# Output projection and routing's row scaling merged into one phase pipelined by tile, with the first expert weights loaded during attention

## The chip, the cores and the metric

One Trainium2 chip, one of its cores. The metric is device time in microseconds of one execution of the whole program; times shown as a median are over several runs on the chip.

## What is computed

The reference takes x of 4 batches x 1024 rows x 256 features (4096 rows in all, float32) through four layers, each added to its own input: a causal attention with 16 heads of 16 features, a mixture of experts (8 experts, 2 per row, hidden size 512), a second attention with one head of 256 features, and the same mixture of experts again:

```python
x = x + attn_a(layernorm(x))      # 16 heads of 16, causal, over 1024 rows of a batch
x = x + ffn(layernorm(x))         # rms norm, top 2 of 8 experts, swiglu 256 -> 512 -> 256
x = x + attn_b(layernorm(x))      # one head of 256, not causal, output layernorm
x = x + ffn(layernorm(x))
```

The part that the change touches lies between the first attention and the first experts: the heads' rows are divided by their softmax sums, multiplied by `Wo` and added to x; then x is normalised (n), x becomes x + n (the outer and the inner residual of the layer), and t = n x (rms scale) x `norm_scale` is what the experts and the router read; the router's logits are t times an 8-column matrix.

## The kernel before

The rows are held as 32 tiles of 128 rows in `g["X"]`, [128, 32, 256], in on-chip memory from start to end. The program is a row of phases (`phase` in `program`, from L1908); each is a block in which every engine has its own instruction list, and the next begins when all engines have ended the last. In time order: `project_qkv`, `attend_a`, `project_out`, `scale_rows`, `rank`, `experts`, then `layer_b`, `rank`, `experts` for the other two layers.

`attend_a` (L361) goes through U = 16 units of four heads and one batch, with a loop (`rotating`, L69). SyncE (SP) issues, in step u: the six head loads of unit u+2 (`load_heads`, L106), then the copy of that unit's V from `g["V"]` into one of three buffers `Vst` (`load_v`, L408), then, once VectorE has the row maxima of unit u+1, three small DMAs that put them into `Qst` (`max_rows`, L414). Each head load is split in three parts of n = 3, 2, 1 (`Q_RUNS`): K and Q are stored as bfloat16 parts, and a Q part is repeated n times by a broadcast on the DRAM side:

```python
q_part = qk_dram[0, bass.ds(u, 1), r * DK:(r + 1) * DK, :, :].rearrange("u d h t -> u d (h t)")   # L109
sp.dma_start(g["Qst"][c * DK:(c + n) * DK, s, :, :].rearrange("p h t -> p (h t)"),                # L112
             q_part.broadcast_to([n, DK, HG * S])).then_inc(g["kq_in"], 16)
```

ScalarE stores each unit's result to `o_dram`, [16 units, 128, 1024]: four heads of 32 rows each, of which 17 hold something, the 16 features and the softmax sum.

`project_out` (L628) takes one tile a step. SP loads the tile's [128, 4, 128] block of `o_dram` into one of two buffers `Ot` (L654), waiting for the transposes two tiles back; in every second step it also issues one piece of each expert matrix, 512 KB of the first (`w1`, L658) and 256 KB of the second (`w2`, L661). TensorE makes four 128 x 128 transposes (L688), VectorE takes the inverse of the sums (L717) and multiplies (L719), TensorE transposes again (L673), ScalarE copies (L704), TensorE multiplies by `Wo` (L679), VectorE adds into X (L712) and takes the statistics (L724); their aggregates for all 32 tiles come at the end (L736).

`scale_rows` (L739) starts with two roots on ScalarE (L777) for all tiles at once, and then per tile: n on VectorE (L806), t on VectorE (L814), x + n on POOL (L852), two transposes of t (L840), a copy on ScalarE (L781), and the logits on TensorE (L830). SP stores t and x in groups of four tiles (L763, L766) and one more tile (L768).

`rank` (L855) starts by loading the gate's bias (L900) and computes on VectorE which row goes to which expert. `experts` (L1058) waits for all expert weights before its first product.

## Time and profile before

| what | us |
|---|---|
| median of 3 runs | 1978.02 |
| lowest and highest of them | 1974.34, 1983.2 |
| the profiled execution's own time | 1974.66 |
| span of its trace | 1972.9 |

The profile is of one execution of its own. Its rows are read as follows: an engine's busy time is the time in which it had an instruction under way; the clock (PEclk) is the clock granted to TensorE as a share of 2.4 GHz; the DMA share is the mean busy share of the core's 16 DMA engines. Rows by line give the count, the busy time, the mean of one, and behind the second bar the idle time just ahead of them on their engine with what ended it.

### The profile page before, as it was taken

To read this page: it belongs to the slowest core of one execution; us is meant where nothing else is said; L and a number is where in the kernel's file an instruction comes from. 1 tells how busy PE (TensorE), PEld (TensorE's weight loads), DVE (VectorE), ACT (ScalarE), POOL (GpSimd) and SP (SyncE) were. 2 spreads that over 40 slices of the span, in tenths; PEclk is the share of its full clock that TensorE was granted. 3 is DMA by queue.
4 is the path that set the end of the run, shared out by engine and by line. 5 is a ranking of instruction groups with operands and counts; after the bars stand their busy time and mean duration, and the time that the engine had idled before them with its cause. 6 is when DMAs were issued, how large, how long until landed. Compare 5 with 4: busy or idle time off the path is not lost. (4 is left out here: it accounts for less than half of the span.)

```text
span 1972.9 us, 32641 instructions
## 1 busy us (share of the span) xinstructions
PE 1750.6 (89%) x8298; PEld 974.6 (49%) x8299; DVE 1341.7 (68%) x2703; ACT 809.7 (41%) x1644; POOL 792.7 (40%) x773
## 2 busy tenths in 40 slices
PE   6979999999998567599999999599975799999997
PEld 3533443444342457266666666344543466666664
DVE  4648888888783357677777777348887567676774
ACT  2424666666666113033333333346761233333332
POOL 4331111111111005156666666134540466666663
PEclk9988999999999895599999999799985899999998
DMA  4662332433320675322222222400113222222222
GB/s 127 161 140 74 94 99 71 100 84 80 98 69 17 209 233 187 123 46 43 47 44 46 43 48 43 109 1 7 58 65 131 56 43 48 43 45 45 47 43 29
DMA packets 116268, 152.83 MB, mean 77 GB/s; under 512 B 17696, under 2 KB 98336, under 8 KB 113120
## 3 DMA queue, kind: packets, MB, share of 16 engines
q1 hardware_dynamic: 79776, 106.28, 19.3%
q0 software_dynamic: 31808, 37.32, 11.8%
q10 hardware_dynamic: 4608, 8.39, 1.2%
q8 instruction: 26, 0.43, 0.1%
q14 instruction: 50, 0.41, 0.1%
HBM read 86.47 MB, written 56.69 MB: 73 GB/s over the span
## 5 line engine op out<-in xcount | busy, mean ns | idle before, releaser
L501 DVE TENSOR_REDUCE a_mx<-a_p_sn 128x1 f32<-128x512 f32 (+3 forms) x640 | 371.2, 632 | 88.6 <-PE a_p_sn L540 61.4
L474 ACT ACTIVATE a_Pt<-a_p_st 128x512 f32<-128x512 f32 (+2 forms) x624 | 306.3, 576 | 191.2 <-PE a_p_st L554 177.1
L1202 ACT ACTIVATE e_y<-e_yb,e_wt 128x256 f32<-128x256 f32 x142 | 72.2, 508 | 505.7 <-DVE e_yb L1229 503.0
L1162 PE MATMUL e_p_y<-w,e_hT 128*128 x1136 | 270.4, 381 | 2.0 <-ACT e_hT L1196 2.0
L1141 PE MATMUL e_p_g<-w,e_tT 128*128 x568 | 270.7, 599 | 0.0
L1141 PE MATMUL e_p_l<-w,e_tT 128*128 x568 | 267.9, 594 | 0.0
L1162 PEld LDWEIGHTS e_p_y<-w,e_hT 128*128 128x128 f32 x1136 | 216.2, 191 | 92.4 <-issue 66.7
L537 PE MATMUL a_p_sn<-Kst,Qst 96*128 96x512 bf16 (+3 forms) x768 | 248.0, 343 | 7.2 <-DMA Qst<-qk_parts 5.7
L450 POOL TENSOR_SCALAR_AFFINE_SELECT a_Pt<-a_Pt 128x512 f32<-128x512 f32 x128 | 81.6, 637 | 418.7 <-ACT a_Pt L474 418.7
L554 PE MATMUL a_p_st<-Qst,Kst 99*128 99x512 bf16 (+3 forms) x768 | 214.4, 332 | 15.2 <-ACT a_Pt L474 12.5
L1053 POOL DMA_INDIRECT xs<-t_rows,token x142 | 143.5, 1011 | 134.5 <-DVE r_used L1006 83.7
L1246 DVE TENSOR_TENSOR e_lin<-e_p_l,R 128x512 f32<-128x512 f32 x142 | 98.2, 692 | 111.6 <-PE e_p_l L1141 111.6
L1242 DVE TENSOR_TENSOR e_glu<-e_p_g,R 128x512 f32<-128x512 f32 x142 | 98.2, 692 | 110.5 <-PE e_p_g L1141 89.0
L1105 POOL DMA_INDIRECT e_wt<-pick_weights,pick x142 | 153.3, 1080 | 48.3 <-issue 42.7
L1113 POOL DMA_INDIRECT x_rows<-e_y,result x71 | 115.0, 1620 | 121.7 <-ACT e_y L1202 118.6
L1113 POOL DMA_INDIRECT out<-e_y,result x71 | 115.0, 1620 | 120.1 <-ACT e_y L1202 120.1
L569 PE MATMUL a_p_o<-a_Pt,a_Vst 128*32 128x512 f32 (+3 forms) x1536 | 160.8, 500 | 0.9 <-POOL a_Pt L450 0.9
L537 PEld LDWEIGHTS a_p_sn<-Kst,Qst 96*128 96x128 bf16 x768 | 75.8, 99 | 147.3 <-DVE a_mx L501 118.3
L1141 PEld LDWEIGHTS e_p_g<-w,e_tT 128*128 128x128 f32 x568 | 98.0, 192 | 69.3 <-issue 69.0
L1141 PEld LDWEIGHTS e_p_l<-w,e_tT 128*128 128x128 f32 x568 | 97.4, 191 | 70.0 <-issue 70.0
L554 PEld LDWEIGHTS a_p_st<-Qst,Kst 99*128 99x128 bf16 x768 | 68.9, 98 | 111.7 <-ACT a_Pt L474 77.5
L1785 PE MATMUL b_p_s<-b_nT,b_gT 128*128 128x512 f32 x256 | 117.9, 607 | 2.8 <-ACT b_p_s L1457 2.8
(211 smaller groups left out, 2534.8 us busy)
## 6 DMA issues: line engine op xcount, KB each, us to landing
qk_parts<-a_part SPq DMA_DIRECT2D x64, 192.0 KB, 2.7
a_Vst<-V SPq DMA_DIRECT2D x16, 512.0 KB, 16.5
o_rows<-a_OT ACTq DMA_DIRECT2D x32, 256.0 KB, 2.1
a_Ot<-o_rows SPq DMA_DIRECT2D x32, 256.0 KB, 3.4
w<-in_mlp SPq DMA_DIRECT2D x16, 512.0 KB, 4.2
R<-in_mlp_b SPq DMA_DIRECT2D x16, 512.0 KB, 8.2
Kst<-qk_parts SPq DMA_DIRECT2D x16, 384.0 KB
Qst<-qk_parts SPq DMA_DIRECT2D x16, 384.0 KB
```

The lines of the kernel that those rows point to most:

```text
L474: act.activation(weights(kb, slice(h, h + n), a, b), p_st[:, i % RING, 0:n * (b - a)].rearrange("p (n w) -> p n w", n=n), ACT.Exp, scale=D ...
L501: dve.tensor_reduce(mx[:, hs[0]:hs[-1] + 1, place], p_sn[:, (s + k) % RING, 0:w * len(hs)].rearrange("p (h w) -> p h w", w=w), AX.X, ALU.m ...
L537: mm = pe.matmul(out, Qst[0:ROWS, s, h, qb * P:(qb + 1) * P], Kst[0:ROWS, s, h, k0:k0 + kw], start=True, stop=True, skip_group_check=True)
L554: mm = pe.matmul(p_st[:, i % RING, j * (b - a):(j + 1) * (b - a)], Kst[0:ROWS + MROWS, s, h0 + j, kb * P:(kb + 1) * P], Qst[0:ROWS + MROWS ...
L569: mm = pe.matmul(p_o[PAD * h:PAD * (h + 1), c, a:512], Vst[:, s, kb, PAD * h:PAD * (h + 1)], weights(kb, h, 512 * c + a, 512 * (c + 1)), s ...
L1053: pool.indirect_dma_start(out=g["xs"][:, j % 2, :], out_offset=None, in_=t_dram, in_offset=bass.IndirectOffsetOnAxis(ap=g["token"][:, j:j ...
L1105: pool.indirect_dma_start(out=wt[:, j:j + 1], out_offset=None, in_=w_dram, in_offset=bass.IndirectOffsetOnAxis(ap=g["pick"][:, j:j + 1], a ...
L1113: pool.indirect_dma_start(out=acc, out_offset=bass.IndirectOffsetOnAxis(ap=g["result"][:, j:j + 1], axis=0), in_=y[:, j % 2, :], in_offset ...
L1141: mm = pe.matmul(bank[:, s, :], tT[:, s, k * P:(k + 1) * P], g["w1"][:, bass.ds(e, 1), k, cols].rearrange("p a n -> p (a n)"), start=(k == ...
L1162: mm = pe.matmul(p_y[:, s, 0:D], hT[:, s, k * P:(k + 1) * P], g["w2"][:, bass.ds(e, 1), k, :].rearrange("p a n -> p (a n)"), start=(k == 0 ...
L1242: dve.tensor_tensor(glu[:, s, :], p_g[:, s, :], bias(0), ALU.add).then_inc(g_read, 1)
L1785: mm = pe.matmul(p_s[:, j % 2, half, :], gT[:, k, q * P:(q + 1) * P], nT[:, b % 2, k, half * 512:(half + 1) * 512], start=(k == 0), stop=( ...
```

## The change

It does four things. The first expert matrix is loaded during attention, one piece of 512 KB a step, into the memory of the V of a unit whose copy has been made: V and `w1` share `g["VW"]`. `project_out` and `scale_rows` become one phase, `out_rows`, in which each engine goes through 41 steps and works on several tiles at different stages in each. The moments, roots and coefficients are taken for groups of four tiles. And n is made by ScalarE from a shift and a factor, not by VectorE. The load of `Ot` now takes two tiles at a time, into one of three buffers, with four DMAs of 17 rows each in place of one of 128.

```diff
@@ -414,6 +414,15 @@
                     sp.dma_start(Qst[ROWS + r:ROWS + r + 1, s, :, :].rearrange("p h (q t) -> p (h q) t", t=P),
                                  mT[r * HG * QB:(r + 1) * HG * QB, :]).then_inc(m_in, 16)
+            def load_w1(u):
+
+                if isinstance(u, int) and u >= U - 2:
+                    sp.wait_ge(v_in, 16 * U)
+                sp.nop(nofuse=True)
+                halves = g["mlp1"].rearrange("e (k p) n -> (e k) p n", p=P)
+                sp.dma_start(g["VW"][:, bass.ds(u, 1), :].rearrange("p u n -> p (u n)"),
+                             halves[bass.ds(u, 1)].rearrange("u p n -> p (u n)")).then_inc(g["w_in"], 16)
+
             load_v(0, 0)
             max_rows(0, 0)
             sp.wait_ge(v_in, 16)
@@ -435,6 +444,7 @@
                     load_v(u + 2, (s + 2) % 3)
                 if not (isinstance(u, int) and u == U - 1):
                     max_rows(u + 1, (s + 1) % 3)
+                load_w1(u)
             rotating(sp, step)
         @block.gpsimd
@@ -625,231 +635,255 @@
-def project_out(nc, mem, g, o_dram):
...
-def scale_rows(nc, mem, g, t_dram, acc):
...
+def out_rows(nc, mem, g, o_dram, t_dram, acc):
...
@@ -1123,7 +1157,7 @@
         @block.tensor
         def _(pe):
-            pe.wait_ge(g["w_in"], 2 * 16 * NT // 2)
+            pe.wait_ge(g["w_in"], 16 * (U + NT // 2))
             def rows(j, s, first):
                 pe.wait_ge(xs_in[s], 16 * (j - s) + 32)
@@ -1918,6 +1952,9 @@
         g["st6"] = keep.sb("st6", [P, NT, 6])
         g["mv"] = keep.sb("mv_all", [P, NT, 2])
         g["mv2"] = keep.sb("mv2_all", [P, NT, 2])
+        g["VW"] = keep.sb("values_then_w1", [P, U, QB * HG * PAD])
+        g["V"] = g["VW"][:, :, :].rearrange("p u (k h c) -> p u k h c", h=HG, c=PAD)
+        g["w1"] = g["VW"][:, :, :].rearrange("p (e k) n -> p e k n", k=KD)
         g["token"] = keep.sb("token", [P, MT], I32)
         g["result"] = keep.sb("result", [P, MT], I32)
         g["pick"] = keep.sb("pick", [P, MT], I32)
@@ -1935,20 +1972,17 @@
         with ExitStack() as heads:
             early = Mem(nc, heads)
-            g["V"] = early.sb("V", [P, U, QB, HG, PAD])
             g["Kst"] = early.sb("Kst", [P, 3, HG, S], BF16)
             g["Qst"] = early.sb("Qst", [P, 3, HG, S], BF16)
             phase(project_qkv, "a1_", a["x"], qk_dram)
             phase(attend_a, "a2_", qk_dram, o_dram)
         g["R"] = keep.sb("R", [P, NT, D])
         g["xs"] = keep.sb("xs", [P, 2, D])
-        g["w1"] = keep.sb("w1", [P, E, KD, 2 * I])
         g["w2"] = keep.sb("w2", [P, E, KI, D])
-        phase(project_out, "a3_", o_dram)
         g["xs_in"] = [keep.sem(f"xs_in1_{s}") for s in range(2)]
         with ExitStack() as span:
             g["p_l"] = Mem(nc, span).ps("p_logits1", [P, 512])
-            phase(scale_rows, "s1_", t_dram, x_dram)
+            phase(out_rows, "a3_", o_dram, t_dram, x_dram)
             phase(rank, "r1_", t_dram, w_dram)
         phase(experts, "e1_", t_dram, w_dram, x_dram, spent, True)
         g["xs_in"] = [keep.sem(f"xs_in2_{s}") for s in range(2)]
```

The new function, with the declarations cut:

```python
def out_rows(nc, mem, g, o_dram, t_dram, acc):
    C = DK + 1
    DEEP, GROUP = 3, 4
    Ot = mem.sb("Ot", [HG * C, DEEP, HG, 2 * P])
    ...
    p_l = g["p_l"]
    STEPS = NT + 9
    def n_of(j):
        return g["R"][:, j % 8, :]
    def t_of(j):
        return g["R"][:, 8 + j % 8, :]
    def x_of(j):
        return g["X"][:, j, :]
    with nc.Block() as block:
        @block.sync
        def _(sp):
            def load(q):
                if q >= DEEP:
                    sp.wait_ge(rows_done, 2 * (q - DEEP) + 2)
                b, at = 2 * q // QB, 2 * q % QB * P
                for h in range(HG):
                    src = o_dram[b * HG:(b + 1) * HG, PAD * h:PAD * h + C, at:at + 2 * P]
                    sp.dma_start(Ot[C * h:C * (h + 1), q % DEEP], src.rearrange("u p t -> p u t")).then_inc(o_in[q % DEEP], 16)
            def load_w2(i):
                e, k = i // 2, i % 2
                sp.dma_start(g["w2"][:, e, 2 * k:2 * k + 2, :], g["mlp2"][e, 2 * k * P:2 * (k + 1) * P, :]
                             .rearrange("(k p) n -> p k n", p=P)).then_inc(g["w_in"], 16)
            def store(c):
                rows = slice(GROUP * c * P, GROUP * (c + 1) * P)
                sp.wait_ge(t_done, GROUP * (c + 1))
                sp.dma_start(t_dram[rows, :].rearrange("(t p) d -> p t d", p=P),
                             g["R"][:, 8 + GROUP * (c % 2):8 + GROUP * (c % 2 + 1), :]).then_inc(t_out[c % 2], 16)
                sp.wait_ge(added, GROUP * (c + 1))
                sp.dma_start(acc[rows, :].rearrange("(t p) d -> p t d", p=P),
                             g["X"][:, GROUP * c:GROUP * (c + 1), :]).then_inc(x_out, 16)
            load(0)
            sp.dma_start(wo[:, :, :], g["WoT"].rearrange("(k p) n -> p k n", p=P)).then_inc(w_in, 16)
            load(1)
            sp.dma_start(srep[:, :], g["scale"].partition_broadcast(P)).then_inc(c_in, 16)
            sp.dma_start(gw[:, :, :], g["gate_w"].rearrange("(k p) e -> p k e", p=P)).then_inc(c_in, 16)
            for j in range(0, STEPS + 4, 2):
                if j // 2 + 2 < NT // 2:
                    load(j // 2 + 2)
                if j // 2 < NT // 2:
                    load_w2(j // 2)
                if j >= 12 and j % 4 == 0 and (j - 12) // 4 < NT // GROUP:
                    store((j - 12) // 4)
            sp.dma_start(acc[T:T + P, :], g["X"][:, 0, :]).then_inc(x_out, 16)
            for s in range(2):
                sp.wait_ge(t_out[s], 16 * (NT // 8))
            sp.wait_ge(x_out, 16 * (NT // GROUP + 1))
        @block.tensor
        def _(pe):
            def rows(j):
                pe.wait_ge(o_in[j // 2 % DEEP], 16 * HG * (j // 2 // DEEP + 1))
                if j >= 2:
                    pe.wait_ge(on_done, j - 1)
                for u in range(HG):
                    mm = pe.transpose(p_r[:, j % 2, u * HG * C:(u + 1) * HG * C],
                                      Ot[:, j // 2 % DEEP, u, j % 2 * P:(j % 2 + 1) * P], g["ident"][0:HG * C, 0:HG * C])
                mm.then_inc(rows_done, 1)
            def turn_out(j):
                pe.wait_ge(on_done, j + 1)
                if j >= 1:
                    pe.wait_ge(onT_done, j)
                for k in range(KD):
                    mm = pe.transpose(p_o[:, k * P:(k + 1) * P], On[:, j % 2, k * P:(k + 1) * P], g["ident"][:, :])
                mm.then_inc(to_done, 1)
            def multiply(j):
                pe.wait_ge(onT_done, j + 1)
                if j >= 2:
                    pe.wait_ge(x_done, j - 1)
                for k in range(KD):
                    mm = pe.matmul(p_x[:, j % 2, 0:D], OnT[:, j % 2, k * P:(k + 1) * P], wo[:, k, :],
                                   start=(k == 0), stop=(k == KD - 1))
                mm.then_inc(px_done, 1)
            def turn(j):
                pe.wait_ge(t_done, j + 1)
                if j >= 2:
                    pe.wait_ge(tT_done, j - 1)
                for k in range(KD):
                    mm = pe.transpose(p_t[:, j % 2, k * P:(k + 1) * P], t_of(j)[:, k * P:(k + 1) * P], g["ident"][:, :])
                mm.then_inc(tp_done, 1)
            def logits(j):
                pe.wait_ge(tT_done, j + 1)
                for k in range(KD):
                    mm = pe.matmul(p_l[:, E * j:E * (j + 1)], tT[:, j % 2, k * P:(k + 1) * P], gw[:, k, :],
                                   start=(k == 0), stop=(k == KD - 1), skip_group_check=True)
                mm.then_inc(l_done, 1)
            pe.wait_ge(w_in, 16)
            pe.wait_ge(c_in, 32)
            for j in range(STEPS):
                if j < NT:
                    rows(j)
                if 0 <= j - 1 < NT:
                    turn_out(j - 1)
                if 0 <= j - 2 < NT:
                    multiply(j - 2)
                if 0 <= j - 7 < NT:
                    turn(j - 7)
                if 0 <= j - 8 < NT:
                    logits(j - 8)
        @block.scalar
        def _(act):
            def out_turned(j):
                act.wait_ge(to_done, j + 1)
                if j >= 2:
                    act.wait_ge(px_done, j - 1)
                act.copy(OnT[:, j % 2, :], p_o[:, 0:D]).then_inc(onT_done, 1)
            def deviations(c):
                at = slice(GROUP * c, GROUP * (c + 1))
                act.wait_ge(mv_done, c + 1)
                act.activation(root[:, 0, at], g["mv"][:, at, 1], ACT.Sqrt, bias=g["eps"][:, :]).then_inc(root_done, 1)
                act.activation(root[:, 1, at], g["mv"][:, at, 1], ACT.Sqrt, bias=g["eps2"][:, :], scale=1.0 + EPS
                               ).then_inc(root_done, 1)
            def normal(j):
                act.wait_ge(coef_done, 2 * (j // GROUP + 1))
                if j >= 8:
                    act.wait_ge(added, j - 7)
                    act.wait_ge(t_done, j - 7)
                act.activation(n_of(j), x_of(j), ACT.Identity, scale=inv[:, 0, j:j + 1], bias=shift[:, j:j + 1]
                               ).then_inc(n_done, 1)
            def turned(j):
                act.wait_ge(tp_done, j + 1)
                if j >= 2:
                    act.wait_ge(l_done, j - 1)
                act.copy(tT[:, j % 2, :], p_t[:, j % 2, 0:D]).then_inc(tT_done, 1)
            for j in range(STEPS):
                if 0 <= j - 1 < NT:
                    out_turned(j - 1)
                if 0 <= j - 6 < NT:
                    normal(j - 6)
                if 0 <= j - 8 < NT:
                    turned(j - 8)
                if j % GROUP == 1 and 0 <= (j - 5) // GROUP < NT // GROUP:
                    deviations((j - 5) // GROUP)
        @block.vector
        def _(dve):
            def inverse_sums(j):
                dve.wait_ge(rows_done, j + 1)
                rows = p_r[:, j % 2, 0:H * C].rearrange("p (h c) -> p h c", c=C)
                dve.reciprocal(rec[:, j % 2, :], rows[:, :, DK]).then_inc(rec_done, 1)
            def attended(j):
                dve.wait_ge(rec_done, j + 1)
                if j >= 2:
                    dve.wait_ge(to_done, j - 1)
                rows = p_r[:, j % 2, 0:H * C].rearrange("p (h c) -> p h c", c=C)
                dve.tensor_tensor(On[:, j % 2, :].rearrange("p (h d) -> p h d", d=DK), rows[:, :, 0:DK],
                                  rec[:, j % 2, :].unsqueeze(2).to_broadcast([P, H, DK]), ALU.mult).then_inc(on_done, 1)
            def add(j):
                dve.wait_ge(px_done, j + 1)
                dve.tensor_tensor(x_of(j), p_x[:, j % 2, 0:D], x_of(j), ALU.add).then_inc(x_done, 1)
            def statistics(j):
                dve.wait_ge(x_done, j + 1)
                ins = dve.bn_stats(g["st6"][:, j, :], x_of(j))
                if j % GROUP == GROUP - 1:
                    ins.then_inc(st_done, 1)
            def moments(c):
                dve.wait_ge(st_done, c + 1)
                for j in range(GROUP * c, GROUP * (c + 1)):
                    ins = dve.bn_aggr(g["mv"][:, j, :], g["st6"][:, j, :])
                ins.then_inc(mv_done, 1)
            def coefficients(c):
                at = slice(GROUP * c, GROUP * (c + 1))
                dve.wait_ge(root_done, 2 * c + 2)
                dve.reciprocal(inv[:, :, at], root[:, :, at]).then_inc(inv_done, 1)
                dve.wait_ge(inv_done, c + 1)
                dve.scalar_tensor_tensor(out=shift[:, at], in0=g["mv"][:, at, 0], scalar=-1.0, in1=inv[:, 0, at],
                                         op0=ALU.mult, op1=ALU.mult).then_inc(coef_done, 1)
                dve.tensor_tensor(inv[:, 1, at], inv[:, 1, at], root[:, 0, at], ALU.mult).then_inc(coef_done, 1)
            def scaled(j):
                dve.wait_ge(n_done, j + 1)
                if j >= 8:
                    dve.wait_ge(tp_done, j - 7)
                    dve.wait_ge(t_out[j // GROUP % 2], 16 * (j // 8))
                dve.scalar_tensor_tensor(out=t_of(j), in0=n_of(j), scalar=inv[:, 1, j:j + 1],
                                         in1=srep[:, :], op0=ALU.mult, op1=ALU.mult).then_inc(t_done, 1)
            dve.wait_ge(c_in, 32)
            for j in range(STEPS):
                if j < NT:
                    inverse_sums(j)
                if 0 <= j - 7 < NT:
                    scaled(j - 7)
                if j < NT:
                    attended(j)
                if j % GROUP == 2 and 0 <= (j - 6) // GROUP < NT // GROUP:
                    coefficients((j - 6) // GROUP)
                if 0 <= j - 2 < NT:
                    add(j - 2)
                    statistics(j - 2)
                if j % GROUP == 1 and 0 <= (j - 5) // GROUP < NT // GROUP:
                    moments((j - 5) // GROUP)
        @block.gpsimd
        def _(pool):
            for j in range(NT):
                pool.wait_ge(n_done, j + 1)
                pool.tensor_tensor(x_of(j), x_of(j), n_of(j), ALU.add).then_inc(added, 1)
```

## Rows read from the trace of the kernel before

**Rows 1.** The profile page: span and busy time of each engine.
```profile
span 1972.9 us, 32641 instructions
...
PE 1750.6 (89%) x8298; PEld 974.6 (49%) x8299; DVE 1341.7 (68%) x2703; ACT 809.7 (41%) x1644; POOL 792.7 (40%) x773
```

**Rows 2.** Windows: attention, output projection, row scaling, ranking; columns in the first line.
```profile
core 0: us, PE busy (x) PEld busy (x) DVE busy (x) ACT busy (x) POOL busy (x), PEclk, DMA share, GB/s
150.00:650.00 500.00, 474.44 (x3544) 191.76 (x3543) 377.28 (x712) 317.88 (x656) 81.58 (x128) 0.98 0.31 78
650.00:740.30 90.30, 57.22 (x320) 46.52 (x320) 47.93 (x160) 11.93 (x33) 0.00 (x0) 0.90 0.77 236
740.30:784.40 44.10, 38.33 (x192) 37.73 (x192) 36.68 (x69) 13.83 (x35) 26.10 (x32) 0.50 0.58 197
784.40:821.40 37.00, 17.65 (x67) 8.96 (x67) 29.62 (x77) 1.77 (x3) 0.00 (x0) 0.50 0.34 115
```

**Rows 3.** Groups by line, 650 to 785 us: busy us, mean ns, idle before.
```profile
L852 POOL TENSOR_TENSOR X<-X,s_n 128x256 f32<-128x256 f32 x32 | 26.1, 835 | 107.9 <-DVE s_t L814 107.9
...
L688 PE MATMUL a_p_r<-ident,a_Ot 128*128 128x128 f32 x128 | 22.6, 304 | 32.2 <-DMA a_Ot<-o_rows 32.2
...
L814 DVE SCALAR_TENSOR_TENSOR s_t<-s_n,s_inv,s_srep 128x256 f32<-128x256 f32 x32 | 13.9, 473 | 0.0
L712 DVE TENSOR_TENSOR X<-a_p_x,X 128x256 f32 (+1 forms) x32 | 13.6, 425 | 6.9 <-PE a_p_x L679 3.9
L719 DVE TENSOR_TENSOR a_On<-a_p_r,a_rec 128x256 f32<-128x256 f32 x32 | 13.6, 425 | 1.1
...
L724 DVE BATCH_NORM_STATS2 st<-X (+1 forms) x29 | 12.2, 422 | 0.0
...
L717 DVE RECIPROCAL a_rec<-a_p_r 128x16 f32<-128x16 f32 x32 | 8.1, 254 | 70.8 <-PE a_p_r L688 70.7
```

**Rows 4.** Timeline where attention ends: start us, duration us, engine, line, operation.
```profile
650.04 0.43 SPq L648 DMA_DIRECT2D a_wo<-in_WoT  x1
650.52 1.38 SPq L654 DMA_DIRECT2D a_Ot<-o_rows  x2
...
654.04 1.09 PE L688 MATMUL a_p_r<-ident,a_Ot 128*128 128x128 f32 x4 [7.24 <-DMA a_Ot<-o_rows]
```

**Rows 5.** Timeline where the row scaling ends and the ranking starts.
```profile
778.76 1.58 POOL L852 TENSOR_TENSOR X<-X,s_n 128x256 f32<-128x256 f32 x2 [0.62 <-DVE s_t L814]
...
784.45 0.34 SPq L900 DMA_DIRECT2D r_gb<-in_gate_b  x1
```

**Rows 6.** Timeline of SyncE's queue for one attention step.
```profile
559.90 0.83 SPq L112 DMA_DIRECT2D Qst<-qk_parts  x1
...
561.39 0.73 SPq L112 DMA_DIRECT2D Qst<-qk_parts  x1
...
564.34 0.58 SPq L408 DMA_DIRECT2D a_Vst<-V  x1
```

**Rows 7.** Windows behind that step's issues; DMA share is of 16 engines.
```profile
565.00:570.00 5.00, 4.62 (x37) 1.76 (x34) 3.65 (x7) 3.50 (x8) 0.78 (x2) 1.00 0.76 177
570.00:575.00 5.00, 5.00 (x37) 1.77 (x33) 4.30 (x7) 3.04 (x6) 0.63 (x1) 1.00 0.19 69
575.00:580.00 5.00, 5.00 (x44) 2.13 (x41) 3.53 (x7) 2.56 (x5) 0.64 (x1) 1.00 0.12 50
```

**Rows 8.** DMA issues, whole execution: count, KB each, median us to landing.
```profile
a_Vst<-V SPq DMA_DIRECT2D x16, 512.0 KB, 16.5
...
w<-in_mlp SPq DMA_DIRECT2D x16, 512.0 KB, 4.2
```

**Rows 9.** DMA queues, 745 to 780 us: packets, MB, share of 16 engines.
```profile
q1 hardware_dynamic: 7392, 7.34, 60.9%
```

**Rows 10.** The same from 660 to 736 us.
```profile
q1 hardware_dynamic: 21005, 19.06, 80.9%
```

**Rows 11.** Waits from 150 to 648 us: total us, times, longest.
```profile
PE a_p_st L554 <- DMA Qst<-a_mT: 0.7, 1, 0.7
```

More of the change, by code:

```diff
@@ L664, in _ @@
-            paired(sp, NT, step)
-        @block.tensor
-        def _(pe):
-            pe.wait_ge(w_in, 16)
-            def turn(j, s):
-                pe.wait_ge(on_done, j + 1)
-                for k in range(KD):
-                    mm = pe.transpose(p_t[:, s, k * P:(k + 1) * P], On[:, s, k * P:(k + 1) * P], g["ident"][:, :])
-                mm.then_inc(t_done, 1)
-            def multiply(j, s):
-                pe.wait_ge(onT_done, j + 1)
-                for k in range(KD):
-                    mm = pe.matmul(p_x[:, s, 0:D], OnT[:, s, k * P:(k + 1) * P], wo[:, k, :],
-                                   start=(k == 0), stop=(k == KD - 1))
-                mm.then_inc(px_done, 1)
-            def step(j, s, first, last):
-                pe.wait_ge(o_in[s], 8 * (j - s) + 16)
-                if not first:
-                    pe.wait_ge(on_done, j - 1)
-                for u in range(HG):
-                    mm = pe.transpose(p_r[:, s, u * P:(u + 1) * P], Ot[:, s, u, :], g["ident"][:, :])
-                mm.then_inc(rows_done, 1)
-                if not (first and s == 0):
-                    turn(j - 1, 1 - s)
-                if not first:
-                    multiply(j - 2, s)
-            paired(pe, NT, step)
-            turn(NT - 1, 1)
-            for t in range(NT - 2, NT):
-                pe.wait_ge(x_done, t - 1)
-                multiply(t, t % 2)
@@ L770, in _ @@
                 sp.wait_ge(t_out[s], 16 * (NT // 8))
-            sp.wait_ge(x_out, 16 * (NT // 4 + 1))
-        @block.scalar
-        def _(act):
-            for r in range(2):
-                act.wait_ge(chain, 1 if r == 0 else 4)
-                act.activation(root[:, r, :], var1[:, :], ACT.Sqrt, bias=g["eps"][:, :]).then_inc(roots, 1)
-            for j in range(NT):
-                act.wait_ge(tp_done, j + 1)
-                act.copy(tT[:, j % 2, :], p_t[:, j % 2, 0:D]).then_inc(tT_done, 1)
```

198 lines of the change are left out of this document (71 added, 127 removed).

## The prediction, written before the changed kernel ran

> **What bounds the kernel now.** I read the page for the span [rows 1], then windows cut where the phases meet [rows 2]. Four stretches matter: the first attention, 650.04 to 740.3 us (output projection), to 784.4 (row scaling), and the ranking, which nothing in the diff touches. The change works on the two in the middle. From the projection's first issued instruction at 650.04 [rows 4] to the ranking's first at 784.45 [rows 5] they take 134.4 us.
>
> The groups by line [rows 3] say what each waits for. In the projection TensorE idled 32.2 us before the transposes of L688, released by the DMA into `Ot`, while the DMA engines were 77% busy at 236 GB/s [rows 2]: it is bound by transfers. In the scaling the DMA share is 58%, and TensorE is busy 38.33 of 44.10 us at a granted clock of 0.50, the lower of its two levels (1.2 of 2.4 GHz); it had been at 0.90 before. So an ordinary reading is: take the expert weights out of the transfer-bound phase, lay the two phases over each other, and win some tens of microseconds.
>
> The next view changes that. In every middle step of attention SyncE issues six head loads and one copy of V. Two of the six are `Qst` loads by L112 whose DRAM side is `broadcast_to([n, DK, HG*S])` with n = 3 and n = 2 [rows 6]. After all are issued the DMA share is 0.76, then 0.19, then 0.12 [rows 7]. Sixteen times 0.19 is 3.0 engines, sixteen times 0.12 is 1.9. So long after the others have finished, three engines and then two still work: just as many as n, the size of the outermost dimension on the DRAM side. And the V copy, 512 KB over 128 partitions, issued last, lands after 16.5 us, where an equal weight load lands after 4.2 [rows 8]: its share on the slow engines stands behind their backlog. If the two loads had gone to different engines, five would have been busy together. They use the same ones. The number is what one gets from the largest count up to 16 that divides the outermost dimension of both sides (48 and 3 give 3, 32 and 2 give 2, 128 and 128 give 16).
>
> The Trainium skill says this outright ("DMA: Bandwidth & Descriptors", section "Why a DMA increments its semaphore by 16 and not by 1"): the issuing side takes the largest k up to 16 that divides both slowest dimensions, on the lowest-numbered engines, and 127 partitions get one. By that, the trace agrees; by it the two phases take the 250 us worked out below, and without it the 106 of the first rival.
>
> **The change part by part.** The new `Ot` load reads only 17 of each head's 32 rows: four DMAs for two tiles, each [17, 4, 256 floats] on both sides. 17 is prime and shares no divisor with 16. So each of the four runs on one engine, and all four on the same one. That is the term that decides.
>
> *Load on that engine.* A load moves 4 x 17 x 4 = 272 pieces of 1 KB. There are 16 loads: 4352 pieces. Ahead of the last one the same engine also has its sixteenth of what is spread over all: `wo` 16, `srep` 8, thirteen of the sixteen `w2` loads 13 x 16 = 208, four pairs of stores 4 x 64 = 256. Sum 4840 pieces; `gw`'s 16 pieces of 32 bytes I leave at nothing.
>
> *Price of a piece.* From 745 to 780 us only 1 KB pieces moved: 7.34 MB in 60.9% of 16 x 35 us = 341 us of engine time, 47.6 ns per 1024 bytes [rows 9]. From 660 to 736, with half-size pieces in the mix, 19.06 MB took 80.9% of 16 x 76 = 984 us, or 52.9 ns [rows 10]: the upper bound. The two engines alone from 575 to 580 moved 50 GB/s, 26 GB/s each, with much larger pieces: 39.4 ns [rows 7], the lower bound. I take 47.6, the row with pieces of this size. 4840 x 47.6 = 230.4 us; the bounds are 190.7 and 255.8.
>
> *Is the engine ever idle?* Three buffers are in turn. `load(q)` waits for the transposes of pair q-3, which come within a few us of that pair's landing; two loads, some 26 us of work, are then still queued. So it is always fed. It even delays the start: TensorE first waits for `srep` and `gw`, which stand behind two loads on that engine, (544 + 24) x 47.6 ns = 27 us. That lies beside the 230.4 and costs nothing more.
>
> *The ends.* First issue to first piece about 1.5 us, and as much from the last piece to its semaphore (`wo`, issued at 650.04, let TensorE start at 654.0 [rows 4]). Behind the last landing: two tiles' transposes at the low clock 2.2 us (1.09 each, [rows 4]); three VectorE steps up to the statistics of tile 31, 5.2 (three times the 2.0 us that its five operations of one tile take in rows 3, less what has run out); the last group's moments, roots and coefficients 1.4; the first ScalarE pass 0.5; four POOL additions 4 x 0.835 = 3.3 [rows 3]; from the last addition to the ranking 4.1 (778.76 + 1.58 to 784.45, [rows 5]). Sum 16.7. The small ones are estimates, a few operations of 0.2 to 0.5 us each; an error there is worth a microsecond or two.
>
> *Phase:* 1.5 + 230.4 + 1.5 + 16.7 = 250.1 us, against 134.4: +115.7.
>
> *What the compute costs.* Per tile VectorE has 254 + 425 + 425 + 422 + 473 ns [rows 3] and a quarter of each group's small operations, about 0.3 us: 2.3 us. TensorE at the low clock needs some 4.4 us (1.8 x 0.90/0.50 + 1.2, from rows 2), ScalarE (11.93 + 13.83)/32 = 0.8 and one pass more, POOL 0.84. A pair of tiles gets (4840 x 47.6 ns)/16 = 14.4 us. All of it is covered, and the merged phases, the removed barrier and the lower clock are all worth nothing, since the loads hide them. If that cover goes, they decide (first rival).
>
> *w1 in attention.* Sixteen loads of 512 KB, 4.2 us each to land [rows 8], one per step of about 30 us. Each is issued behind the max rows, and the next head loads follow some 2 us later; it adds 32 KB, about 1.3 us, to each engine's queue. Behind it on SP stand the next head and V loads, needed most of a step later. TensorE waited for a transfer into `Qst` 0.7 us in all here [rows 11]. Bounds: 0, and 16 x 1.3 = 21 us if each were exposed. I take 0, by the last row. SyncE's own issue time (0.58 us for the V copy, [rows 6]) fits its wait. Ranking and experts are untouched: 0.
>
> **Sum.** Against the profiled execution: 1974.66 + 115.7 = 2090.4 us. The median of the runs shown, 1978.02, is 3.4 above that execution, so the forecast is 2093.7, say 2093. Bounds on the same base: 4840 x 39.4 gives 2054, 4840 x 52.9 gives 2119.
>
> **Rivals.** *The loads spread* (the other side: faster). If the four DMAs of a load each took another engine, a piece of 68 KB would take 68 x 47.6 ns = 3.2 us, or less if each were spread wider, and two tiles of compute take longer than that. It decides from the point where a load uses two engines for its four parts or more: one engine is 14.4 us per pair, four are about 4. Then compute sets the pace: VectorE 2.3 us; TensorE 57.22/32 = 1.8 for the projection and half of the 38.33/32 = 1.2 that it now needs for scaling, 2.4 [rows 2]; plus, once in four tiles, the chain of roots and coefficients through ScalarE. I put 2.6 us (2.3 to 2.9). Phase: 7 for the start (eleven issues before `gw`), 32 x 2.6 = 83, 16 at the end: 106, or 28 less than now, 1950 us. For it: the phase was transfer-bound and loses w1's 8.4 MB and half of `Ot`'s bytes. Against it: shares 0.19 and 0.12.
>
> *The loads spread, but TensorE stays at the low clock* as in the scaling phase (0.50 while 87% busy). Then a tile costs about 1.8 x 0.90/0.50 + 1.2 = 4.4 us, the phase 7 + 141 + 16 = 164, +30: 2008 us. Against: all that the engine does in the projection, at 0.90, stays in the mix.
>
> *A lone engine is not the same pace*: faster because fifteen others leave memory free, or slower because a read's latency shows. That is the range of the forecast, not another outcome.
>
> **Chances.** One engine 0.91; spread 0.07; spread at low clock 0.02. A measurement can tell about 0.5%, 10 us. Faster 0.07, same 0.01, slower 0.92. The range takes the forecast's bounds, the lower a little in and the upper a little out, since a read's latency adds and hardly subtracts: 2060 to 2126. Of the forecast's 0.91 some 0.1 lies outside; the rivals are left out.
>
> **What would show it.** In the after trace: a phase of some 250 us with a DMA share near 0.1 (one engine of 16, plus stores) and 25 to 45 GB/s; TensorE idle before the transposes of `Ot`, released by the DMA; the first transpose some 27 us into the phase; pairs of tiles every 14.4 us; each `Ot` DMA of 68 KB landing after tens of us. Attention keeps its 500 us. I am wrong on the mechanism if that share is above 0.4 and tiles come every 2 to 3 us; wrong on the size if a pair takes under 12 or over 16 us.

## The result and the profile after

The changed kernel took 2098.93 us (median of 4 runs, 2098.38 to 2099.58) against 1977.99 for the kernel before (4 runs, 1974.34 to 1983.2) on the same chip: ratio 1.0598, 95% interval 1.058 to 1.0617. It is slower, 5.9 us above the 2093 forecast. The profiled execution took 2099.12 us.

The page of the kernel after has the same engines with almost the same busy times as before [rows 1], in a longer span. The merged phase fills the thirteenth to the eighteenth slice (52.4 us each); there the clock line is at 5 and 6 tenths.

```profile
span 2097.4 us, 32382 instructions
...
PE 1778.0 (85%) x8298; PEld 992.5 (47%) x8299; DVE 1323.7 (63%) x2690; ACT 827.1 (39%) x1690; POOL 782.9 (37%) x773
...
PEclk9978999999996555558999999979996599999998
DMA  4644434434410112333222222230113222222222
```

The windows after, cut where attention ends (first issue of the merged phase), where ranking starts, and where ranking ends, answer to [rows 2]:

```profile
core 0: us, PE busy (x) PEld busy (x) DVE busy (x) ACT busy (x) POOL busy (x), PEclk, DMA share, GB/s
150.00:657.70 507.70, 482.41 (x3550) 194.06 (x3548) 379.51 (x715) 318.50 (x656) 81.47 (x128) 0.96 0.36 94
657.70:909.10 251.40, 116.14 (x512) 97.71 (x512) 65.52 (x216) 42.73 (x113) 23.54 (x32) 0.57 0.22 70
909.10:946.10 37.00, 17.65 (x67) 8.97 (x67) 29.64 (x77) 1.77 (x3) 0.00 (x0) 0.50 0.34 115
```

The merged phase takes 251.4 us where the two phases took 134.4: +117.0. Attention ends 7.7 us later (657.74 against 650.04), and from ranking's first issue to the end it is 1188.2 us, against 1188.5. Together, 117.0 + 7.7 less 0.2, that is the difference of the spans, 124.5 (2097.4 - 1972.9). In the phase no engine is busy for half the time. Two windows inside it, before the first product and in steady state:

```profile
660.00:680.00 20.00, 0.00 (x0) 0.00 (x0) 0.00 (x0) 0.00 (x0) 0.00 (x0) 0.50 0.12 35
710.00:730.00 20.00, 9.01 (x38) 7.57 (x39) 5.20 (x17) 2.98 (x7) 2.17 (x3) 0.59 0.10 34
```

A share of 0.10 is 1.6 of 16 engines: one that never stops and the `w2` pieces that pass over all of them. The groups by line of the phase say who waits, to be held against L688 in [rows 3] (32.2 us there):

```profile
L729 PE MATMUL a_p_r<-ident,a_Ot 68*128 68x68 f32 x128 | 21.5, 323 | 93.2 <-DMA a_Ot<-o_rows 60.9 <-DMA a_gw<-in_gate_w 32.3
```

The timeline gives the start, a steady stretch of SyncE's queue, and the last pair's first transposes (columns as in [rows 4]):

```profile
657.74 6.00 SPq L689 DMA_DIRECT2D a_Ot<-o_rows  x4
...
686.83 1.14 PE L729 MATMUL a_p_r<-ident,a_Ot 68*128 68x68 f32 x8 [32.30 <-DMA a_gw<-in_gate_w]
...
706.58 10.41 SPq L689 DMA_DIRECT2D a_Ot<-o_rows  x4
717.03 3.18 SPq L693 DMA_DIRECT2D w<-in_mlp  x1
720.25 10.35 SPq L689 DMA_DIRECT2D a_Ot<-o_rows  x4
730.64 3.18 SPq L693 DMA_DIRECT2D w<-in_mlp  x1
...
885.27 0.72 PE L729 MATMUL a_p_r<-ident,a_Ot 68*128 68x68 f32 x4 [4.95 <-DMA a_Ot<-o_rows]
...
909.17 0.34 SPq L934 DMA_DIRECT2D r_gb<-in_gate_b  x1
```

Between stores a pair comes every 13.7 us (706.58 to 720.25); from the first group of stores on it is 14.8 on average, a group of stores for every two pairs included. The first product starts 29.1 us into the phase, the last pair's first 227.5 us into it, and 23.9 us follow.

### The profile page after: what moved, and what is told of

Same layout as the page of the kernel before. It is cut to its first block and busy times, and to the rows that moved or that the text cites. A ratio compares the mean times of both kernels' runs of the same rounds, so it can differ in the third digit from the quotient of the medians.

```text
span 2097.4 us, 32382 instructions
## 1 busy us (share of the span) xinstructions
PE 1778.0 (85%) x8298; PEld 992.5 (47%) x8299; DVE 1323.7 (63%) x2690; ACT 827.1 (39%) x1690; POOL 782.9 (37%) x773
## 5 line engine op out<-in xcount | busy, mean ns | idle before, releaser
L1175 PE MATMUL e_p_g<-values_then_w,e_tT 128*128 x568 | 270.2, 598 | 0.0
L1175 PE MATMUL e_p_l<-values_then_w,e_tT 128*128 x568 | 267.5, 593 | 0.0
L1139 POOL DMA_INDIRECT e_wt<-pick_weights,pick x142 | 148.6, 1046 | 48.2 <-issue 42.7
L1175 PEld LDWEIGHTS e_p_g<-values_then_w,e_tT 128*128 128x128 f32 x568 | 98.1, 193 | 69.1 <-issue 69.0
L1175 PEld LDWEIGHTS e_p_l<-values_then_w,e_tT 128*128 128x128 f32 x568 | 97.3, 191 | 69.7 <-issue 69.7
```

The costliest lines, as they stand in the source:

```text
L1139: pool.indirect_dma_start(out=wt[:, j:j + 1], out_offset=None, in_=w_dram, in_offset=bass.IndirectOffsetOnAxis(ap=g["pick"][:, j:j + 1], a ...
L1175: mm = pe.matmul(bank[:, s, :], tT[:, s, k * P:(k + 1) * P], g["w1"][:, bass.ds(e, 1), k, cols].rearrange("p a n -> p (a n)"), start=(k == ...
```

## Experiments

The theory is that a load of 17 rows runs on one DMA engine, which carries all 64 of them. Its rivals are that the merged phase is slow for another reason (its depth, the low clock, the start behind the constants), and that the bytes or the row count as such matter. In kernels with more rows per head, the extra rows of `Ot` are transposed too and not read. Each run is compared with runs of the kernel before on the same chip.

**Rows per head: 18, 19, 32.** One number changes, here to 18, in the two others to 19 and 32.

```diff
-    C = DK + 1
+    C = 18
```

> The changed kernel with 18 rows per head in each Ot load in place of 17: one more row of bytes, the same four DMAs. Theory A (a load runs on as many engines as the largest count up to 16 that divides the outermost dimension of both sides): 18 gives 9 engines, 32 + 48 pieces of 1 KB on the busiest per pair of tiles, 3.7 us; compute sets the pace, a pair comes every 5 to 6 us, the merged phase takes 100 to 115 us and the time is 1945 to 1965 us. Theory B (four small DMAs in place of one large, or rows of a few partitions, are slow by themselves): a pair still takes 13 to 15 us, the time is 2100 to 2115 us.

> The changed kernel with 19 rows per head. Theory A: 19 is prime, so one engine as with 17, with 19/17 of the pieces: 512 more, at 47 ns each +24 us, 2118 to 2128 us. Theory B: two more rows of bytes are 12% more, the same direction, +20 to +30 us; this run prices a piece, and only together with the 18 rows does it tell the theories apart, since by B 18 lies between 17 and 19.

> The changed kernel with all 32 rows per head, padding too: still four DMAs, now of 32 partitions. Theory A: 16 engines, 32 + 48 pieces on each per pair, phase 100 to 115 us, 1945 to 1965 us; within 10 us of the run with 18 rows, although it moves 1.8 times its Ot bytes. Theory B (bytes or number of DMAs decide): not faster than the run with 18 rows by more than noise, and both above 2100 us.

Measured, before 1981.57: 18 rows 1949.09 us, ratio 0.9838 (0.9813 to 0.9864); 19 rows 2121.68, ratio 1.0716 (1.0685 to 1.0748); 32 rows 1949.94, ratio 0.9847 (0.9825 to 0.987). One row more takes 150 us away, the next puts it back with 23 on top, and 32 rows cost the same as 18. The number of rows by itself decides nothing; its divisors do. The largest number up to 16 that divides both sides is 1 for 17 and 19, 9 for 18 and 16 for 32. The expectations were met by all three, 1949.09 and 1949.94 in 1945 to 1965 and 2121.68 in 2118 to 2128. Two windows of the kernel with 18 rows, the phase and a steady stretch of it, and two lines of SyncE's timeline:

```profile
core 0: us, PE busy (x) PEld busy (x) DVE busy (x) ACT busy (x) POOL busy (x), PEclk, DMA share, GB/s
655.10:755.70 100.60, 76.70 (x512) 64.05 (x512) 64.61 (x216) 41.67 (x113) 23.84 (x32) 0.88 0.58 179
...
695.00:705.00 10.00, 8.89 (x64) 7.33 (x64) 7.47 (x27) 4.71 (x15) 2.90 (x4) 1.00 0.71 226
...
696.32 1.39 SPq L689 DMA_DIRECT2D a_Ot<-o_rows  x4
697.75 0.39 SPq L693 DMA_DIRECT2D w<-in_mlp  x1
```

In 10 us there are 64 of the 512 products, 4 of 32 tiles: 2.5 us a tile, with TensorE busy 89% at the full clock. How many engines a load uses can be read before the first product, where little else is under way. Four windows in which hardly anything but pieces of `Ot` moved: the changed kernel (17 rows), 18 rows, 32 rows, and the kernel cut another way, which comes next.

```profile
664.00:666.00 2.00, 0.00 (x0) 0.00 (x0) 0.00 (x0) 0.00 (x0) 0.00 (x0) 0.50 0.07 23
```

```profile
661.20:662.20 1.00, 0.00 (x0) 0.00 (x0) 0.00 (x0) 0.00 (x0) 0.00 (x0) 0.50 0.57 146
```

```profile
662.00:663.00 1.00, 0.00 (x0) 0.00 (x0) 0.00 (x0) 0.00 (x0) 0.00 (x0) 0.50 0.93 155
```

```profile
661.20:662.70 1.50, 0.00 (x0) 0.00 (x0) 0.00 (x0) 0.00 (x0) 0.00 (x0) 0.50 0.28 85
```

Sixteen times these shares is 1.1, 9.1, 14.9 and 4.5, against the 1, 9, 16 and 4 of the theory. The second also rules out a near rule that 17, 19 and 32 rows would fit as well, the common divisor with 16: 18 rows would then run on two engines, and two moved 50 GB/s [rows 7], not 146. The phase with 32 rows takes 105.4 us, 4.8 more than with 18. The depth of the pipeline, its stages and the number of DMAs are the same in all these kernels, so none of them is what made the merged phase slow; nor is the low clock, which is back at 1.00 in the steady stretch. The window of the phase with 19 rows prices the lone engine again:

```profile
657.10:929.30 272.20, 114.30 (x512) 96.04 (x512) 65.53 (x216) 42.59 (x113) 23.80 (x32) 0.59 0.21 67
```

The two further rows add 2 x 4 x 4 x 16 = 512 pieces to the 4840 and 20.9 us to the phase (272.3 by its first issues): 41 ns for each added one.

**The same 17 rows, cut another way.** Each of the four DMAs takes one unit with its four heads, so that the outermost dimension is 4 on the DRAM side and 68 on the chip's.

```diff
-                for h in range(HG):
-                    src = o_dram[b * HG:(b + 1) * HG, PAD * h:PAD * h + C, at:at + 2 * P]
-                    sp.dma_start(Ot[C * h:C * (h + 1), q % DEEP], src.rearrange("u p t -> p u t")).then_inc(o_in[q % DEEP], 16)
+                for u in range(HG):
+                    src = o_dram[b * HG + u, :, at:at + 2 * P].rearrange("(h c) t -> h c t", c=PAD)[:, 0:C, :]
+                    sp.dma_start(Ot[:, q % DEEP, u], src).then_inc(o_in[q % DEEP], 16)
```

> The changed kernel with the same 17 rows and the same 272 pieces of 1 KB per pair, cut by unit in place of by head: each of the four DMAs is [4 heads, 17 rows, 256] on the DRAM side and [68 partitions, 256] on chip. Theory A: 4 divides 4 and 68, so four engines, 68 + 48 pieces on the busiest per pair, 5.4 us, just about the pace of compute: 1950 to 1975 us. Theory B (number, size and bytes of the DMAs are as in the changed kernel): 2090 to 2105 us.

Measured: 1944.84 us (2 runs), ratio 0.9823 (0.9794 to 0.9852), phase 103.0 us. Bytes, pieces, number of DMAs and compute are those of the changed kernel; the shape alone is worth 148 us of the phase (251.4 less 103.0). The time is 5 us under the range expected (1950 to 1975).

**The start.** The gate's weights, `wo` and the scale go ahead of the second `Ot` load.

```diff
+            sp.dma_start(gw[:, :, :], g["gate_w"].rearrange("(k p) e -> p k e", p=P)).then_inc(c_in, 16)
             load(0)
             sp.dma_start(wo[:, :, :], g["WoT"].rearrange("(k p) n -> p k n", p=P)).then_inc(w_in, 16)
-            load(1)
             sp.dma_start(srep[:, :], g["scale"].partition_broadcast(P)).then_inc(c_in, 16)
-            sp.dma_start(gw[:, :, :], g["gate_w"].rearrange("(k p) e -> p k e", p=P)).then_inc(c_in, 16)
+            load(1)
```

> The changed kernel with 17 rows, and the constants moved: gw ahead of all Ot loads, wo and srep behind the first, the second load last. The theory (one engine works without a pause from the first load to the last, so the wait of 27 us at the start costs nothing by itself): TensorE starts some 12 us earlier, and the time stays within 5 us of the changed kernel, 2094 to 2104 us. Rival (the late start is part of the loss): 2085 to 2089 us.

Measured: 2100.45 us, ratio 1.0603 (1.0585 to 1.0621), phase 252.5. The timeline of this kernel has the first product 16.9 us into the phase (654.73), 12.2 us sooner than in the changed kernel, and nothing came of it (the time is in the range expected, 2094 to 2104):

```profile
654.73 0.39 SPq L705 DMA_DIRECT2D a_gw<-in_gate_w  x1
...
671.59 1.14 PE L729 MATMUL a_p_r<-ident,a_Ot 68*128 68x68 f32 x8 [20.08 <-DMA a_srep<-in_scale]
```

**w1 alone.** The kernel before with only `load_w1` and its memory from the change, so that the projection loads `w2` alone:

```diff
                     max_rows(u + 1, (s + 1) % 3)
+                load_w1(u)
             rotating(sp, step)
...
-                    sp.dma_start(g["w1"][:, bass.ds(e, 1), bass.ds(k, 1), :].rearrange("p e k n -> p (e k n)"),
-                                 g["mlp1"][bass.ds(e, 1), bass.ds(k * P, P), :].rearrange("e p n -> p (e n)")
-                                 ).then_inc(g["w_in"], 16)
```

> The kernel before with one part of the change: w1 loaded in attention into V's place, the output projection and the row scaling as they were. Projection loses 8.4 of its 21 MB; it was transfer-bound, so its 90 us become 60 to 66, the scaling keeps 44. Attention: by my sum 0; by the traces of the changed kernel and its variants, where the middle steps are the same and steps in which a loop turns are up to 4 us longer, 0 to 8 more. Time 1948 to 1960 us. If attention is paid in full for each load (16 x 1.3 us), it gives back 21 us and the time is 1968 or more.

Measured: 1972.62 us against 1982.23, ratio 0.995 (0.9933 to 0.9966). The expectation (1948 to 1960) missed. The two phases took 122.6 us, only 11.9 less, where 104 to 110 had been expected, and attention took 10.0 more, so that almost nothing was left in the profiled execution. The same stretch of the projection, 700 to 720 us, first in the kernel with `w1` alone, then before:

```profile
700.00:720.00 20.00, 16.29 (x100) 13.09 (x100) 13.74 (x39) 3.73 (x10) 0.00 (x0) 1.00 0.64 188
```

```profile
700.00:720.00 20.00, 13.03 (x80) 10.62 (x80) 11.35 (x33) 2.98 (x8) 0.00 (x0) 1.00 0.85 264
```

A tile has 10 products, so the two are 2.0 and 2.5 us a tile. A share of 0.64 is no longer full, yet TensorE still waits for `Ot`: in the stretch 650 to 750 us the waits of the kernel with `w1` alone give

```profile
PE a_p_r L695 <- DMA a_Ot<-o_rows: 21.6, 18, 7.3
```

that is 21.6 us in all, 18 times, the first of 7.3 us at the start. A load is issued only when the buffer two tiles back is free, so part of what the phase saved in bytes seems to have stayed as the time from issue to landing. That is a reading: no run gives this phase a third buffer.

**Where w1 goes, with 18 rows.** One kernel loads `w1` beside `w2` in the merged phase, none in attention. Another loads each piece a second time, into memory that nothing reads; there SyncE also waits for the second load of the step before (lines not shown).

```diff
                 if j // 2 < NT // 2:
+                    load_w1(j // 2)
                     load_w2(j // 2)
```

> The kernel with 18 rows per head and w1 loaded beside w2 in the merged phase, none of it in attention. Theory (attention pays 0 to 6 us for w1, and the merged phase, bound by TensorE at 2.5 us a tile, has room for 512 KB more per pair): attention 518 to 519 us from its first head load, phase 100 to 110 us, 1944 to 1956 us, about the same as with 18 rows. Rival (the merged phase becomes bound by transfers again, 1.57 MB per pair at 236 GB/s are 6.7 us): phase 120 us or more, over 1960 us.

```diff
                              halves[bass.ds(u, 1)].rearrange("u p n -> p (u n)")).then_inc(g["w_in"], 16)
+                sp.dma_start(Wx[:, :], halves[bass.ds(u, 1)].rearrange("u p n -> p (u n)")).then_inc(wx_in, 16)
```

> The kernel with 18 rows per head, and a second load of the same 512 KB behind each w1 load in attention, into a buffer that nothing reads. If w1 costs attention its 4 to 6 us by standing before the loop turns, a second one costs as much again or more, all in steps in which the loop turns: 1952 to 1960 us. If the spread of the turns is chance, the time stays within 3 us of the run with 18 rows.

Measured: beside `w2` 1953.89 us, ratio 0.986 (0.9841 to 0.9878); twice 1953.89, ratio 0.9855 (0.9826 to 0.9884). Both intervals overlap that of the kernel with 18 rows (0.9813 to 0.9864). The phase with `w1` in it is 106.9 us, 6.3 longer; its window:

```profile
652.20:759.10 106.90, 81.38 (x512) 67.92 (x512) 64.75 (x216) 41.86 (x114) 24.00 (x32) 0.84 0.82 247
```

Against that stands attention. The table gives, from one profile each: attention from its second run of head loads (the first is issued much earlier) to the next phase's first issue; in it the three steps in which the loop of `rotating` turns, from head load to head load; and what lies behind the last head load.

| kernel | w1 in attention | attention, us | three turning steps | behind the last head load |
|---|---|---|---|---|
| before | no | 518.6 | 96.2 | 90.7 |
| 18 rows, `w1` beside `w2` | no | 519.1 | 96.6 | 90.6 |
| after | once | 524.8 | 100.0 | 92.8 |
| 18 rows | once | 524.7 | 102.8 | 90.6 |
| 19 rows | once | 524.5 | 99.8 | 92.7 |
| 32 rows | once | 522.2 | 99.7 | 90.5 |
| cut by unit | once | 518.7 | 96.0 | 90.4 |
| `w1` alone | once | 528.6 | 103.6 | 93.0 |
| constants first | once | 522.1 | 99.7 | 90.5 |
| 18 rows, constants first, `w1` earlier (below) | once | 522.5 | 99.2 | 91.3 |
| 18 rows, `w1` twice | twice | 529.0 | 104.6 | 91.3 |
| head loads spread (below) | no | 523.3 | 96.1 | 93.4 |
| all together (below) | once | 520.9 | 93.7 | 92.9 |

So in these profiles `w1` in attention, loaded once, costs 0 to 10 us, 4 to 6 in most, and gives about as much back in the phase behind. The eleven other steps together agree within about 1 us (331.3 to 332.3; 333.2 with `w1` twice, 333.8 and 334.3 in the two last rows, where the second run of head loads is issued 8 to 9 us sooner). Profiles also differ by some us where nothing was changed: from ranking's first issue to the end they took 1185.3 to 1192.3 us. At a turn the engines stop briefly; before, TensorE had nothing under way from 316 to 317 us. The timelines of before and after at the first of them:

```profile
316.45 5.21 ACT L474 ACTIVATE a_Pt<-a_p_st 128x512 f32<-128x512 f32 x11 [2.46 <-issue]
```

```profile
319.09 4.16 ACT L484 ACTIVATE a_Pt<-a_p_st 128x512 f32<-128x512 f32 x8 [3.32 <-issue]
```

ScalarE's stop, for which no data is to blame ("issue"), grows from 2.46 to 3.32 us. TensorE's granted clock was 1.00 from 319 to 325 us before; in the windows behind the turn of the kernel after it is 0.63 and 0.51:

```profile
321.00:323.00 2.00, 2.00 (x14) 0.98 (x13) 1.92 (x4) 1.98 (x5) 0.00 (x0) 0.63 0.38 49
323.00:325.00 2.00, 2.00 (x15) 0.94 (x15) 1.04 (x2) 0.90 (x3) 0.64 (x1) 0.51 0.20 61
```

Where the changed kernel's 6.2 us lie is shown: 3.7 in the turns, 2.2 behind the last head load, 0.3 elsewhere. Why is argued: instructions fetched behind a larger load would explain it, and the order of the three cases (without, once, twice) fits on the whole, but the kernel cut by unit, with the same attention, does not show the cost, so this stays open.

**Constants first and w1 earlier, with 18 rows.** The edit of the start from above, and `load_w1(u)` moved ahead of `max_rows`.

```diff
                     load_v(u + 2, (s + 2) % 3)
+                load_w1(u)
                 if not (isinstance(u, int) and u == U - 1):
                     max_rows(u + 1, (s + 1) % 3)
-                load_w1(u)
```

> The kernel with 18 rows per head, the constants moved ahead as in the other run, and w1 issued right behind the V copy of its step in place of just before the loop turns. With nine engines per load the phase is bound by TensorE, so its start counts now: 4 to 6 us less than with 18 rows alone. If the longer loop turns come from w1 standing in front of what the turn needs, attention gives 2 to 5 us more: 1938 to 1944 us. If they have another cause, attention stays and the time is 1943 to 1946 us.

Measured: 1944.93 us, ratio 0.9807 (0.979 to 0.9824), phase 99.5. The earlier start gave 1.1 us of phase, less than the 4 to 6 expected: the first product came 6.7 us into it (661.00) where it had been 8.2 (663.39), and both kernels ran their first tiles at a granted clock of 0.50. The three turning steps took 99.2 us, between the 96.2 without `w1` and the 102.8 with it issued later, so the order of issue settles nothing there. The interval overlaps that of 18 rows alone.

**The head loads spread.** The kernel before, with each broadcast of n = 3 or 2 replaced by n loads of 16 partitions (the count that is waited for follows).

```diff
-        sp.dma_start(g["Qst"][c * DK:(c + n) * DK, s, :, :].rearrange("p h t -> p (h t)"),
-                     q_part.broadcast_to([n, DK, HG * S])).then_inc(g["kq_in"], 16)
+        for i in range(c, c + n):
+            sp.dma_start(g["Qst"][i * DK:(i + 1) * DK, s, :, :].rearrange("p h t -> p (h t)"),
+                         q_part.rearrange("u d n -> (u d) n")).then_inc(g["kq_in"], 16)
```

> The kernel before with one edit in attention: each Qst load of n = 3 or 2 repeats becomes n loads of 16 partitions, so that 16 divides both sides; bytes and pieces are the same. Theory (the number of engines is the largest common divisor up to 16): the stretch with 2 to 3 of 16 engines busy goes, the DMA share behind the issues stays over 0.5 until all has landed and then is near 0, and the V copy lands after 5 to 10 us in place of 16.5. Rival (the broadcast is slow for another reason, its rows of 8 KB): the copy still lands after 14 us or more. Time: same, or up to 10 us less if the fetches at the loop turns stood behind the backlog.

Measured: 1973.22 us (10 runs) against 1982.57 (15 runs), ratio 0.9963 (0.9947 to 0.9978). The windows of this kernel at the place of [rows 7], and its row for the copy of V from the DMA issues:

```profile
560.00:565.00 5.00, 4.87 (x36) 1.71 (x33) 3.15 (x6) 2.77 (x7) 0.64 (x1) 1.00 1.02 142
565.00:570.00 5.00, 5.00 (x35) 1.73 (x35) 4.37 (x8) 3.04 (x8) 0.64 (x1) 1.00 0.33 122
570.00:575.00 5.00, 5.00 (x54) 2.42 (x55) 3.88 (x7) 3.13 (x8) 0.64 (x1) 1.00 0.00 0
```

```profile
a_Vst<-V SPq DMA_DIRECT2D x16, 512.0 KB, 9.5
```

The tail of shares 0.19 and 0.12 is gone, and V lands after 9.5 us where it took 16.5 [rows 8]. So the tail was those broadcasts. The time that this gave does not come from attention's steady steps, which TensorE fills anyway (the three turning ones take 96.1 us, as before), but from the start. Behind the first run of head loads SyncE has 16 stores of Q and K to issue, and this takes it 19.65 us where it took 28.80:

```profile
102.77 19.65 SPq L172 DMA_DIRECT2D qk_parts<-a_part  x16
```

```profile
102.64 28.80 SPq L171 DMA_DIRECT2D qk_parts<-a_part  x16
```

The second run of head loads is issued at 122.46 us where it was 131.49. Of these 9.0 us about half is left at the end of attention: the next phase starts at 645.78 instead of 650.04.

**All together.** 18 rows, constants first, `w1` ahead of the max rows, head loads spread.

> All that paid put together: 18 rows per head, constants first, w1 behind the V copy, and the split head loads. If the backlog on engines 0 to 2 is what makes the loop turns in attention long, their steps go from 31 to 35 us to about 30 to 31 and the time to 1925 to 1940 us; if it is not, 1940 to 1946 us as without the split.

Measured: 1934.33 us (5 runs, 1933.36 to 1937.99), ratio 0.9766 (0.9742 to 0.9791), against the same 1982.57. It beats both kernels: 2.3% below the one before, some 8% below the changed one (0.9766 / 1.0598 = 0.921), as expected (1925 to 1940). Its three turning steps take 93.7 us, with `w1` in attention; the kernel without the spread head loads and otherwise the same took 99.2. So the backlog of the broadcasts had a part in the long turns, as far as one profile of each can tell. Its merged phase:

```profile
644.60:744.10 99.50, 77.27 (x512) 64.31 (x512) 64.59 (x216) 41.73 (x114) 23.87 (x32) 0.88 0.60 181
```

## Why the prediction was right, step by step

**The mechanism** held as put. The reading of shares 0.19 and 0.12 as three and two engines, and of the engine count as the largest number up to 16 that divides both outermost dimensions, forecast every case: 17 and 19 rows give one engine, 18 give nine, 32 give sixteen, the same 17 rows cut 4 against 68 give four. (The prediction also says of 17 that it "shares no divisor with 16". That is true and beside the point: 18 shares only 2 with 16, and the window with 18 rows shows 9.1 engines.) That is also the rule of the Trainium skill ("DMA: Bandwidth & Descriptors", section "Why a DMA increments its semaphore by 16 and not by 1"); by it the traces agree, with 251.4 and 272.3 us for the phase at one engine, 103.0 at four, 100.6 at nine and 105.4 at sixteen. That all four DMAs of a load take the same engine is shown by the pitch: 13.7 us for a pair of tiles, where four engines beside each other would have needed a quarter.

**The load and its price.** 4840 pieces at 47.6 ns were to take 230.4 us. The last pair's first product came 227.5 us in; without the 3 us of the two ends, that is 224.5 / 4840 = 46.4 ns. The row with 1 KB pieces alone [rows 9] was the right one, 5.9 us too high; both bounds would have been worse. A pair every 14.4 us was forecast, the stores' share in it; 13.7 was measured between stores, 14.8 with them.

**The start** was to be 27 us, hidden: 29.1 measured, and taking 12.2 of them away changed the phase from 251.4 to 252.5 us. Hidden it was.

**The tail** was the term of the phase that was mis-sized: 16.7 us in the sum, 23.9 measured. By the timeline: 3.9 us from the last landing to the last tile's transposes (2.2 in the sum, as if nothing stood between the two tiles, but TensorE at the low clock works off the other stages of the pipeline there), 8.5 to the last statistics (5.2), 1.5, 0.7 and 3.3 for coefficients, the first pass and the four additions (1.4, 0.5, 3.3), 6.0 to the ranking (4.1). Together 7.2 too little, which the cheaper pieces gave back: the phase was 251.4 against 250.1. That two misses of 6 and 7 us cancel is luck.

**w1 in attention** was taken as 0, and this is the term that was off most, though inside its bounds of 0 to 21. Attention ended 7.7 us later, 1.5 of it from before its second run of head loads (132.96 against 131.49), 3.7 in the three turning steps, 2.2 behind the last head load. The row of [rows 11] said that TensorE hardly waited for a transfer; it could not say what the loop's turns would cost. The forecast was 8.7 us below the profiled execution: 7.7 from here, 1.3 from the phase, less 0.3 behind it. Against the median it was only 5.9 below, since the 3.4 us added because the median before lies above its profiled execution had no counterpart: the changed kernel's median is 0.2 below its own.

**The compute** was rightly called covered. Of the first rival, 18 rows show the numbers: 2.5 us a tile (2.6 forecast), a phase of 100.6 (106) and 1949.09 us (1950). That the time came so close is chance, as the phase is 5 us shorter and attention ended 5 us later than that sum had it. The second rival, the low clock for the whole phase at 4.4 us a tile, did not come: 1.00 in the steady window. The low clock in the changed kernel's phase (0.57) goes with its idleness: the same number of products packed into 100.6 us had 0.88.

**The worth of the change's parts.** The merge alone, with loads that spread and `w1` beside `w2`, gives 1953.89 us, the ratio 0.986; adding `w1` in attention gives no difference that these intervals tell. `w1` in attention without the merge gives 0.995. The shape of one load turns the sum of them into 1.0598.

## What to carry to other kernels

Before shortening a DMA to fewer rows, look at the outermost dimension of both sides, a broadcast's included, and at the largest number up to 16 that divides both: a load of useful rows alone (17) lost 150 us to one with a useless row more (18). In a trace such a load shows as a DMA share near a small multiple of 1/16 beside compute that waits for a transfer. A pipeline can be sized from the old trace only after asking whether its new loads spread.

## What the runs showed of the hardware that was not expected

**The queue that issues is held too.** SyncE needs 10.4 us for the four `Ot` issues and 2.8 to 3.2 for one `w2` issue behind them, which itself moves over all engines; with 18 rows it is 1.39 and 0.39. With 19 rows the `w2` issue takes up to 3.55. The 28.80 us for the stores of Q and K, above, show it behind the broadcasts too. So a lone engine's backlog stops everything behind it on SyncE, the spread loads and stores too. In the merged phase nothing else was urgent there: the stores are the one case, with VectorE waiting 43.2 us for them in four waits, beside the time in which it would have waited for tiles anyway.

```profile
DVE R L863 <- DMA t_rows<-R: 43.2, 4, 11.2
```

This is a row of the waits of the changed kernel, 650 to 905 us: total, times, longest.

**A lone engine is about as fast as one of sixteen.** Its 46.4 ns a piece lies close to the 47.6 of sixteen at 61% [rows 9]. The comparison is rough: that row is of stores, the lone engine mostly loads, and the 512 added pieces of the kernel with 19 rows came at 41 ns each. Fifteen idle engines made the one faster by somewhere between nothing and 15%, which changes nothing here.
